# A decoder layer on one Trainium2 core: every second block of sigmoids rounded by ScalarE, PSUM banks emptied in pairs, and split activations kept in DRAM for the upper product

## The reference

```python
def act_qdq(x):
    qmax = 2.0 ** (ACT_BITS - 1) - 1.0
    scale = jnp.maximum(jnp.max(jnp.abs(x)) / qmax, 1e-12)
    return jnp.clip(jnp.round(x / scale), -qmax - 1.0, qmax) * scale

def fixed_qdq_u16(x):
    scale = 1.0 / 65536.0
    return jnp.clip(jnp.round(x / scale), 0.0, 65535.0) * scale
...
x = act_qdq(x)
up = act_qdq(x @ lpbq_dequant(w_up).T)
gate = act_qdq(x @ lpbq_dequant(w_gate).T)
sig = fixed_qdq_u16(jax.nn.sigmoid(gate))
gate = act_qdq(gate * sig)
o = act_qdq(gate * up)
return o @ lpbq_dequant(w_down).T
```

## Time and profile before

| | |
|---|---|
| median of 3 runs | 1463.64 us (1463.39, 1463.64, 1465.57) |
| the profiled execution, its own time | 1462.73 us |
| its span, first to last instruction | 1460.9 us |
| busy in the span | PE 1287.5, DVE 1060.1, ACT 949.9, POOL 355.3 us |
| mean granted TensorE clock | 0.948 |
| gate product (first to last L1895 on `raw`'s banks) | 1133.0 to 1200.7 us |
| sigmoid stage (`inv` of gate to the step of up and the product) | 1203.7 to 1306.7 us |

### The profile page before, as it was taken

The page is one execution under the profiler, slowest core; times in us unless marked ns, Lnnn a source line. Parts: engine busy times, 40 slices in busy tenths (PEclk is TensorE's granted clock), DMA queues, the critical chain, the costliest instruction groups (busy, mean ns, idle before and its releaser), DMA issues. The chain is left out here.

```text
span 1460.9 us, 24914 instructions
## 1 busy us (share of the span) xinstructions
PE 1287.5 (88%) x8220; PEld 686.1 (47%) x8220; DVE 1060.1 (73%) x2557; ACT 949.9 (65%) x1666; POOL 355.3 (24%) x593
## 2 busy tenths in 40 slices
PE   7788999999999999999999999989985998800597
PEld 4344344334334434434433433437874887600486
DVE  4376887887887887887788788743663568999655
ACT  4444777777777777777777777764674559749600
POOL 4544211211212112121121121113551006600012
PEclk9988999999999999999999999999996999965799
DMA  8999978878698697787887877425411003315032
GB/s 246 299 336 268 237 205 232 222 225 217 198 257 211 196 253 212 214 226 202 239 223 216 220 209 225 138 89 164 104 57 44 1 0 130 154 46 217 1 115 87
DMA packets 260302, 260.54 MB, mean 178 GB/s; under 512 B 65838, under 2 KB 246606, under 8 KB 256078
## 3 DMA queue, kind: packets, MB, share of 16 engines
q1 hardware_dynamic: 258542, 255.81, 60.7%
q10 hardware_dynamic: 1632, 3.15, 0.7%
HBM read 147.40 MB, written 110.71 MB: 177 GB/s over the span
## 5 line engine op out<-in xcount | busy, mean ns | idle before, releaser
L603 ACT ACTIVATE pr<-scoresT 128x512 f32<-128x512 f32 x1024 | 550.7, 600 | 222.8 <-PE scoresT L851 162.8
L847 PE MATMUL scoresT<-qT,kT 99*128 99x512 bf16 (+7 forms) x1408 | 359.3, 326 | 5.3 <-DVE attn_out L740 2.3
L695 DVE CUSTOM_DVE_ANT_0 junk<-scores_for_max,win 128x200 f32<-128x200 f32 (+2 forms) x512 | 179.9, 351 | 172.0 <-PE scores_for_max L822 161.3
L700 DVE TENSOR_REDUCE mx<-scores_for_max 128x1 f32<-128x888 f32 (+6 forms) x448 | 301.6, 673 | 0.0
L698 DVE TENSOR_REDUCE mx<-scores_for_max 128x1 f32<-128x64 f32 (+6 forms) x448 | 277.3, 619 | 0.0
L864 PE MATMUL attn_out<-pr,vS 128*17 128x512 f32 x2048 | 270.3, 600 | 4.4 <-DMA vS<-v_all 4.2
L847 PEld LDWEIGHTS scoresT<-qT,kT 99*128 99x128 bf16 (+1 forms) x1408 | 113.8, 97 | 335.0 <-ACT rows L580 97.0
L851 PE MATMUL scoresT<-idf,win 128*128 128x128 f32 x1024 | 218.9, 275 | 0.0
L477 POOL COPY rows<-rows 128x736 f32<-128x736 f32 x128 | 102.1, 798 | 390.0 <-ACT rows L580 390.0
L821 PE MATMUL scores_for_max<-kX,qT 64*128 64x512 bf16 x512 | 165.1, 385 | 4.3 <-DVE mx L700 3.0
L822 PE MATMUL scores_for_max<-kX,qX 64*128 64x512 bf16 x512 | 165.1, 385 | 0.0
(11 more groups left out here) (205 smaller groups left out, 1798.0 us busy)
## 6 DMA issues: line engine op xcount, KB each, us to landing
rel_table<-rows SPq DMA_DIRECT2D x128, 512.0 KB, 4.5
win<-rel_table SPq DMA_DIRECT2D x128, 512.0 KB, 5.4
up_raw<-xT_normed SPq DMA_DIRECT2D x6, 1536.0 KB, 5.1
xT_normed<-up_raw SPq DMA_DIRECT2D x6, 1536.0 KB, 7.2
qT<-q_parts SPq DMA_DIRECT2D x32, 256.0 KB, 7.5
kX<-k_parts SPq DMA_DIRECT2D x64, 128.0 KB, 4.9
kT<-k_parts SPq DMA_DIRECT2D x32, 256.0 KB, 5.5
q_parts<-shared SPq DMA_DIRECT2D x32, 192.0 KB, 4.7
```

The lines of the kernel that those rows point to most:

```text
L603: nc.scalar.activation(pr[:, n % NPR, h, :], bank, ACT.Exp).then_inc(t_read, 1)
L695: last = nc.vector.tensor_tensor_reduce(junk[:, n % 2, 0:z - a], bank[:, a:z], win[:, T % NW, q4, h, u:u + z - a], 1.0, NEG, ALU.add, ALU. ...
L700: last = nc.vector.tensor_reduce(mx[:, T % 2, q4, h, 2:3], bank[:, z:L], AX.X, ALU.max)
L847: last = mm(bank[:, a:e], k[0:r], q[0:r, a:e], start=(n == 0), stop=not near and n == len(pieces) - 1, skip_group_check=True)
```

## The change

Four edits, all in `feed_forward`.

- `empty` takes two neighbouring banks, 128 x 1024, with one instruction; it waits until both are full. Gate and up are both emptied so, three instructions for a block in place of six. Of an upper block one pair is emptied ahead of `round_gate(n + 1)` and two behind it, where it was three and three banks.
- In blocks 1, 3, 5 and 7 (`BY_ACT`) ScalarE rounds the sigmoid itself, right behind `sigmoid(n)`, from `raw` into a second buffer for rounded sigmoids in `shared`, where `xi` stood. VectorE only multiplies in these blocks.
- GpSimd's `split_again` is gone. In the gate stage SP stores `xh` and `xl` of blocks 0 to 5 in DRAM (`xd`, `x_parts`), and in the sigmoid stage loads them again (`load_parts`). `split_rows` gets a wait, that the stores from its buffer have ended.
- On SP the loads of the parts stand among the stores of the upper blocks: the load for block j + 3 is written ahead of the wait and store of block j.

```diff
@@ feed_forward
+    BY_ACT = [n for n in range(NBLK) if n % 2]
...
+        sig = [si[:], shared[:, 0:FT * HALF // 2].bitcast(U16T)]
...
         @block.sync
         def _(sp):
+            def load_parts(j):
+                n = UP[j]
+                sp.wait_ge(f_full, M_ALL + FT * (j - 1))
+                for k, t in enumerate((xh, xl)):
+                    sp.dma_start(whole(t, n), xd[n, k]).then_inc(x_ld[n % 2], 16)
+
+            for n in range(NBLK - 2):
+                sp.wait_ge(f_xg, n + 1)
+                for k, t in enumerate((xh, xl)):
+                    sp.dma_start(xd[n, k], whole(t, n)).then_inc(x_st[n % 2], 16)
+            for j in range(2):
+                sp.wait_ge(x_st[j], 16 * (NBLK - 2))
+            load_parts(2)
             for j in range(NBLK - 2):
+                if j + 3 < NBLK:
+                    load_parts(j + 3)
                 sp.wait_ge(f_out, M_ALL + FT * (j + 1))
                 sp.dma_start(ud[j], ub[j % 2]).then_inc(u_st[j % 2], 16)
-            sp.wait_ge(f_xu, 2 * (NBLK - 2))
...
         @block.gpsimd
-            for j in range(2, NBLK):
-                split_again(j)
...
         @block.scalar
             def empty(k, to):
-                act.wait_ge(f_full, k + 1)
-                nc.scalar.activation(to, ps[:, k % BANKS, :], ACT.Identity, scale=step[:, 0:1]).then_inc(f_out, 1)
+                act.wait_ge(f_full, k + 2)
+                nc.scalar.activation(to.rearrange("p (a n) -> p a n", a=2), ps[:, k % BANKS:k % BANKS + 2, :], ACT.Identity,
+                                     scale=step[:, 0:1]).then_inc(f_out, 2)
...
-            empty_up(0, 0, FT // 2)
+            empty_up(0, 0, 2)
             act.wait_ge(t_inv, 2)
             round_gate(0)
             for n in range(NBLK):
                 sigmoid(n)
+                if n in BY_ACT:
+                    act.wait_ge(f_sig, handed(n, 2))
+                    act.wait_ge(f_xg, NBLK)
+                    if n >= 2:
+                        act.wait_ge(f_g2, handed(n - 2, 2))
+                    nc.scalar.activation(sig[n % 2], raw[:, n, :], ACT.Identity, scale=U16).then_inc(f_sa, 1)
                 if n:
-                    empty_up(n, 0, FT // 2)
+                    empty_up(n, 0, 2)
                 if n + 1 < NBLK:
                     round_gate(n + 1)
-                empty_up(n, FT // 2, FT)
+                empty_up(n, 2, FT)
...
         @block.vector
                 if n >= 2:
                     dve.wait_ge(f_full, FT * (n - 1))
+                    dve.wait_ge(x_st[n % 2], 32 * (n // 2))
...
-                    dve.wait_ge(f_sig, handed(n, t))
-                    nc.vector.tensor_scalar(si[:, c], raw[:, n, c], U16, None, ALU.mult).then_inc(f_si, 1)
-                    dve.wait_ge(f_si, handed(n, t))
-                    nc.vector.tensor_tensor(raw[:, n, c], gi[n % 2][:, c], si[:, c], ALU.mult).then_inc(f_g2, 1)
+                    if n in BY_ACT:
+                        dve.wait_ge(f_sa, BY_ACT.index(n) + 1)
+                    else:
+                        dve.wait_ge(f_sig, handed(n, t))
+                        nc.vector.tensor_scalar(sig[n % 2][:, c], raw[:, n, c], U16, None, ALU.mult).then_inc(f_si, 1)
+                        dve.wait_ge(f_si, handed(n, t) - sum(m < n for m in BY_ACT))
+                    nc.vector.tensor_tensor(raw[:, n, c], gi[n % 2][:, c], sig[n % 2][:, c], ALU.mult).then_inc(f_g2, 1)
...
         @block.tensor
                 if j >= 2:
-                    pe.wait_ge(f_xu, 2 * (j - 1))
+                    pe.wait_ge(x_ld[UP[j] % 2], 32 * (j // 2))
```

More of the change, by code:

```diff
@@ L962, in decoder_rest @@
     ud = nc.dram_tensor("up_raw", [NBLK, P, FT * HALF], F32, kind="Internal").ap()
+    xd = nc.dram_tensor("x_parts", [NBLK - 2, 2, P, 2 * HALF], F32, kind="Internal").ap()
     with ExitStack() as ctx:
@@ L1063, in decoder_rest @@
                         norm_stats, norm_rstd, norm_scalar, largest_of, scale_of, scale_pool)
-        feed_forward(nc, sem, spare, shared, h2d, ud, wgh, wgl, wuh, wul, wdT, xr, ps, magic, coarse, step, inv, t_inv, amax,
+        feed_forward(nc, sem, spare, shared, h2d, ud, xd, wgh, wgl, wuh, wul, wdT, xr, ps, magic, coarse, step, inv, t_inv, amax,
                      largest_of, scale_of, scale_pool, l_sum, norm_stats, norm_rstd, norm_apply, out)
@@ L1577, in _, with feed_forward @@
                 turn_x(n)
-def feed_forward(nc, sem, spare, shared, h2d, ud, wgh, wgl, wuh, wul, wdT, xr, ps, magic, coarse, step, inv, t_inv, amax,
+def feed_forward(nc, sem, spare, shared, h2d, ud, xd, wgh, wgl, wuh, wul, wdT, xr, ps, magic, coarse, step, inv, t_inv, amax,
                  largest_of, scale_of, scale_pool, l_sum, norm_stats, norm_rstd, norm_apply, out):
@@ L1615, in feed_forward @@
         gi = [gi0, old[:, 2 * FT * HALF:2 * FT * HALF + FT * HALF // 2].bitcast(I16)]
+        sig = [si[:], shared[:, 0:FT * HALF // 2].bitcast(U16T)]
         ui = [si[:].bitcast(I16), old_int[:, 0:FT * HALF]]
-        x_one = old[:, 2 * FT * HALF + FT * HALF // 2:]
         work = ub
@@ L1623, in feed_forward @@
         f_xg = sem("f_xg")
-        f_x1 = sem("f_x1")
-        f_x2 = sem("f_x2")
-        f_xu = sem("f_xu")
+        x_st = [sem(f"x_st{j}") for j in range(2)]
+        x_ld = [sem(f"x_ld{j}") for j in range(2)]
         f_full = sem("f_full")
@@ L1632, in feed_forward @@
         f_si = sem("f_si")
+        f_sa = sem("f_sa")
         f_g2 = sem("f_g2")
@@ L1659, in _, with whole @@
         def _(sp):
+            def whole(t, n):
+                return t[:, n % 2].bitcast(F32).rearrange("p c n -> p (c n)")
+            def load_parts(j):
[10 more added lines that the diff above has]
+            load_parts(2)
             for j in range(NBLK - 2):
+                if j + 3 < NBLK:
+                    load_parts(j + 3)
                 sp.wait_ge(f_out, M_ALL + FT * (j + 1))
                 sp.dma_start(ud[j], ub[j % 2]).then_inc(u_st[j % 2], 16)
-            sp.wait_ge(f_xu, 2 * (NBLK - 2))
             for n in range(2):
@@ L1714, in empty @@
             def empty(k, to):
-                act.wait_ge(f_full, k + 1)
-                nc.scalar.activation(to, ps[:, k % BANKS, :], ACT.Identity, scale=step[:, 0:1]).then_inc(f_out, 1)
+                act.wait_ge(f_full, k + 2)
+                nc.scalar.activation(to.rearrange("p (a n) -> p a n", a=2), ps[:, k % BANKS:k % BANKS + 2, :], ACT.Identity,
+                                     scale=step[:, 0:1]).then_inc(f_out, 2)
             def cols(m):
-                return slice(m * HALF, (m + 1) * HALF)
+                return slice(m * HALF, (m + 2) * HALF)
             def round_gate(n):
@@ L1735, in empty_up @@
                     act.wait_ge(f_umax, j - 1)
-                for m in range(first, last):
+                for m in range(first, last, 2):
                     empty(M_ALL + FT * j + m, ub[j % 2][:, cols(m)])
@@ L1757, in _ @@
                     round_rows(n + 2)
-                for m in range(FT):
+                for m in range(0, FT, 2):
                     empty(FT * n + m, raw[:, n, cols(m)])
             nc.scalar.activation(spare[:], magic[:, 1:2], ACT.Sigmoid)
-            empty_up(0, 0, FT // 2)
+            empty_up(0, 0, 2)
             act.wait_ge(t_inv, 2)
```

## The result

The changed kernel took 1453.18 us, the median of four runs (1452.25 to 1454.75), against 1463.68 us before, 10.5 us less: ratio 0.9928, 95% interval 0.9915 to 0.994. Run again beside three of the experiments it was 9.5 us under the kernel before (1455.13 against 1464.61, ratio 0.9933, 0.992 to 0.9947). The forecast was 1454.4, -9.2 us.

The account below looks back on a forecast made before the run. VectorE was taken to bound the sigmoid stage; start -1.0, pairs of block 0 +0.4, roundings -6.8, GpSimd -3.3 and new wait +1.6 gave -9.1 us (-9.2 followed through), forecast median 1454.4 us, range 1452.5 to 1458.5.

Parts of the forecast that it names:

- The start: Start of the sigmoid stage: ScalarE, emptying in pairs, is free to round gate sooner, -1.0 us.
- GpSimd: Sigmoid stage: with GpSimd's work gone, VectorE's products and a rounding are no longer stretched, -3.3 us (bounds 0 and -3.4).
- The roundings: Blocks 1, 3, 5, 7: VectorE loses four instructions of 1.68 us and the 0.02 behind each, -6.8 us.
- The new wait: Block 1: VectorE waits once for ScalarE's emptying of upper block 1, behind the rounding and gate of block 2, +1.6 us.
- Pairs: Emptying two banks with one ScalarE instruction takes 1.13 us, bounds 1.02 and 1.38; +0.4 us in block 0.
- Sum: Start, pairs of block 0, roundings, GpSimd and new wait together: -9.1 us, or -9.2 by the followed timeline.
- ScalarE keeps ahead: Sigmoid stage after block 1: ScalarE needs 20.0 us per two blocks against VectorE's 21.5, never late again.
- Stores covered: Upper block 0's store leaves at about 1217.4, lands by 1226; ScalarE wants the buffer at about 1230.
- the rival of late transfers: Sigmoid stage: loads and stores in one queue come late; at 16 us the gain is used up, 1464; chance 0.02.
- TensorE's clock: Upper product: granted clock stays near 1; a 1.86 us pause had not lowered it, a 3.67 us one had.
- the rival of a lower clock: TensorE stays at the 1.2 GHz level in the upper product, 31 us more than forecast, about 1485; chance 0.03.
- The rival that the change's gain is eaten by ScalarE: Sigmoid stage: ScalarE becomes the bound, needing 22.0 us per two blocks; sum -6.2, 1457.4 us; chance 0.11.

Follow-up runs that it names:

- parts alone: Changed kernel with all sigmoids rounded on VectorE and one bank per emptying instruction: 1460.47 us, ratio 0.9972 to the kernel before.
- A fifth rounding: Changed kernel, all three pairs of block 1 emptied ahead of rounding gate block 2, ScalarE also rounding block 6's sigmoids: 1450.36 us, again 1452.42.
- block 1 emptied first: Changed kernel with ScalarE emptying all three pairs of upper block 1 ahead of rounding gate block 2: 1453.81 us, ratio 0.9928 to the kernel before.
- the swap in block 0: Kernel with five blocks rounded on ScalarE, VectorE taking the product's largest value before upper block 0's: 1453.39 us, ratio 0.9923 to the kernel before.
- the run again: Changed kernel unaltered, measured once more beside three experiments: 1455.13 us against 1464.61 before, ratio 0.9933.

## Why the prediction was right

Its steps, one by one, in the profiled pair.

- **The start**, -1.0: gate's rounding began 3.87 us after the start of gate's last emptying, where it was 4.81; -0.94. With the two pairs of block 0 the largest value of upper block 0 came 0.66 us sooner, forecast 0.6.
- **GpSimd**, -3.3: parts alone gave -3.3 in the stage.
- **The roundings**, -6.8: they took about 0.3 us more off. A period without one is 9.79 us and not 9.9. The step that was mis-sized is the odd period: I took the product's whole length, 3.36, plus a gap of 0.02. With VectorE's rounding ahead of it a product waits until the rounding has ended; without one it begins about 0.1 us before the row of the largest value ahead of it ends (1241.95 + 3.35 = 1245.30, the product at 1245.21), and adds only 3.27 to the chain. That makes 0.1 in each of the three odd periods counted.
- **The new wait**, +1.6, paid once in block 1: 1.42. The rounding cost ScalarE 2.76 us, the lower bound, where I had taken 2.87. Its factor is a constant and not an operand, and I had priced that very difference for the pairs; it fits, but no run changed the factor alone.
- **Pairs**, 1.13: 1.115.
- **Sum** of the stage: forecast -9.2, measured -9.65; in the time -10.5 and -9.5. The misses of the roundings (0.3) and of the wait (0.2) point the same way, so the sum is not right by errors that cancel.
- **ScalarE keeps ahead**: right, with less room than the sum per two blocks suggests. A fifth rounding fitted, at the end, and with block 1 emptied first and the swap in block 0 VectorE met ScalarE in block 3.
- **Stores covered**, "lands by 1226": this step was wrong in its size. The store of upper block 0 left at 1218.7 and not 1217.4, and took 9.3 us where I had allowed 8 beside the loads, a figure that no row gave. It landed at 1228.0, and ScalarE used its buffer again at 1229.7, so this one was covered, by 1.7 us and not by 4. I had followed no later one: the slowest took 11.6 us, and ScalarE waited 0.59 us for its buffer in block 6, in the run again 0.72 us in block 4. The slowest load took 8.4 us, over the 7.6 that I gave to two, and TensorE waited for none. None of this cost VectorE anything, and doubling the loads cost VectorE nothing, so the rival of late transfers stays far off, but the cover I named was not whole.
- **TensorE's clock**: I said that a pause of 1.86 us had left it alone. In upper block 2 it fell behind a pause of 1.78 us, TensorE's timeline:

```profile
1222.37 0.73 PE L1910 MATMUL banks<-x_high,w_up_low 128*128 128x512 f32 x2 [1.78 <-ACT xT_normed L1720]
1222.93 0.94 PE L1910 MATMUL banks<-x_high,w_up_high 128*128 128x512 f32 x2
1223.67 1.05 PE L1910 MATMUL banks<-x_low,w_up_high 128*128 128x512 f32 x2
...
1262.24 0.73 PE L1910 MATMUL banks<-x_high,w_up_low 128*128 128x512 f32 x2 [1.78 <-ACT xT_normed L1720]
```

Behind an equal pause at 1262 it did not fall, and in the run again it fell behind none of three pauses of 1.78, 1.77 and 1.78 us. One such fall costs TensorE about 1.5 us of the 2.4 us it has to spare in a block, so the rival of a lower clock needed many of them.

The rival that the change's gain is eaten by ScalarE was the right one to fear, and it was out by the price of a pair and of a rounding.

## What to carry to other kernels

Follow the wanted instruction through the order of both engines for the first two or three turns, not only the sum per turn: the steady state had 1.5 us of room on ScalarE, and a wait of 1.4 us stood in block 1 all the same, because one block's emptying was written behind the next block's rounding. Work on GpSimd that is off the path is not free while VectorE multiplies two tensors in SBUF; here it cost 3.3 us of 84, and what each product lost was the rest of the GpSimd instruction that was running. Where single executions scatter by more than an edit is worth, a stretch between two events of the trace that the edit lies in (here good to 0.1 us) decides what medians can't.

## What the runs showed that I had not expected

- The chain of waits named a DMA ahead of a VectorE instruction that has no wait on it, with a row that ended just as the true releaser did. The DMA landed 0.9 us later. With block 1 emptied first the chain prints such a row again, from 1239.65 to VectorE's 1247.90, for a store that took 11.5 us to land. The end of a DMA's row in the chain is no landing.
- Two equal pauses of TensorE, 1.78 us, with and without a fall of its clock behind them in one execution; and a first stretch at 1.2 GHz in the gate product that went with a length of 69.7 us in place of 68.5 in two executions of the same code.
- The loads and stores of this stage could be raised to 392 GB/s, DMA share 1.01, without adding anything to its length.
- A product of VectorE and an instruction of GpSimd that meet don't share: the later one stands still until the other is over. So a product of 3.36 us took up to 4.33, and a cast of 0.61 us up to 3.63. VectorE's rounding, with one tensor as input, and GpSimd's subtraction did the same (1.3 us became 2.82).
